# Gathering edge rows straight into an item's place, without the ring of tiles, in a graph transformer layer

## The chip, the cores and the metric

The kernel runs on one core of a Trainium2 chip. Its engines are TensorE (matrix products and transposes, PE in the rows), VectorE (DVE), ScalarE (ACT), GpSimd (POOL) and SyncE (SP, which here only issues DMAs); a small q behind a name means the engine's instruction queue. The metric is the device time of one execution in microseconds; the time before is the median of three runs.

## The reference

A graph layer over 6250 nodes of 128 features and 100,000 edges, sorted by their destination node. For each node k, q and v are its features times a matrix that its node type picks (eight types, each a mix of four basis matrices). For each edge k and v of its source node go through small matrices of its edge type (8 heads of 16), the score is the product of q at the destination with that k, times a factor of edge type and head; a softmax over the edges of a destination weighs v, the sums go through another matrix by node type, then come a product of the node's own features, a bias, ReLU, the residual and a layer norm:

```python
kt = jnp.einsum('nhi,thij->tnhj', k, relation_att)[edge_type, src]
e = (q[dst] * kt).sum(-1) * relation_pri[edge_type] * scale
a = softmax of e over the edges of one dst
vt = jnp.einsum('nhi,thij->tnhj', v, relation_msg)[edge_type, src]
agg = jax.ops.segment_sum(a[..., None] * vt, dst, num_segments=n)
out = relu(decomp(agg) + node_feat @ loop_weight + bias)
x = layernorm(x + out)
```

## The kernel before

**Table stage.** The nodes are taken in 49 blocks of 128 (a loop of 51 steps in TensorE's program). For each block and each of the eight edge types the finished k and v rows are made, copied out of PSUM by ScalarE (line 1557) into one of four places, and stored by SP (line 1141) in a table in HBM: 50,176 rows of 1 KB, one for each node and edge type. A block's store is 1 MB. ScalarE reuses a place once the store of four blocks earlier has landed. At block 41 SP first waits for five signals of stage 0, the last of which is GpSimd's clearing of agg (line 1435), and issues the loads for the queries (lines 1126, 1117, 1120).

**Setup beside it.** The edges lie in 782 tiles of 128 (784 with padding). A tile whose edges belong to more than one block of destination nodes counts once for each block: such a pair of tile and block is an item. There are 832 places for items, 26 groups of 32. GpSimd and VectorE work out which tile and which block an item has. Index gathers of GpSimd (line 1375, seven of them) fetch the destinations of each item, and TensorE turns two tables so that they lie by column (line 1883, in the steps 34, 35, 37 and 38): the lanes of the items, and the table rows of the tiles' edges, rows_idx. Clearing agg, whose space the first holds, waits for the turning.

**Query stage.** After the table q is made for all nodes by TensorE, ScalarE and VectorE.

**Loop over the groups.** For each item TensorE spreads the queries to the edges with a one-hot matrix, VectorE multiplies them with the k rows (line 686), four items (a batch) at a time, and sums them to scores (line 696); a group later the maxima are found, v is weighed (line 794), TensorE sums by node with the one-hot matrix (line 2084), and VectorE adds the sums to agg (line 845). The rows of the items lie in kv, which holds two groups, 64 items.

**How the rows get there.** GpSimd gathers each tile once, into one of the 16 places of a ring (lines 1448 to 1461). Before a gather it waits for the landing of the gather seven places back and passes that on to SP; for every second one it loads a count from a table and waits until SP has freed the ring's places. SP (bring, lines 1158 to 1175) loads the tile numbers of the batch's four items, waits until the place in kv is free, which is when the batch two groups back is weighed, waits for the tiles to have landed, and copies each item's tile from the ring to its place in kv:

```python
for u in range(4):
    if u == 2 and n > 0:
        sp.wait_ge(s_gathered[(n - 1) // NBATCH % 2][(n - 1) % NBATCH],
                   (n - 1) // (2 * NBATCH) * 64 + 64)
        sp.sem_inc(s_freed, 4)
    if u % 2 == 0:
        sp.wait_ge(s_landed, each[u + 1] & 1023)
        hold_apart(sp)
```

**Last stage.** The sums are normalised, multiplied, and stored. SP issues its loads; the first of these stand between its last copies.

The order on each engine is written out by hand; waits on semaphores join the engines.

Of the kernel before, what the change touches and what calls it, by code (L numbers as in the profile page):

```python
# [5 lines left out]
def graph_transformer_layer(  # L6
# [82 lines left out]
    RING = 16  # L89
    AHEAD = 7  # L90
    TSEMS = 8
    assert AHEAD < TSEMS and RING & (RING - 1) == 0 and GROUPS * G < ITEMS

# [7 lines left out]
    item_block = nc.dram_tensor("item_block", [2, ITEMS], i32, kind="Internal").ap()  # L101

    ctx = ExitStack()
    with ctx:
# [25 lines left out]
        rows_idx = sb("rows_idx", [P, TILES], i32)  # L130
# [4 lines left out]
        itile = strip[32:33, :].bitcast(i32)  # L135
        iblk = strip[64:65, :].bitcast(i32)
        starts_row = strip[96:97, 0:TILES - 1]
        next_start = starts_row.bitcast(i32)
# [6 lines left out]
        ring = sb("ring", [P, RING * 2 * D])  # L145
# [66 lines left out]
        s0i = rows3[:, 0:IPR * P].bitcast(i32)  # L212
        tdst = s0i[0:TROWS, :].rearrange("p (c e) -> p c e", c=TPR)
# [29 lines left out]
        yo = (s3.take(CN), ring[:, 0:CN])  # L243
# [15 lines left out]
        ring_coefs = take_coefs(Space(ring, RING * 2 * D, at=CN), HALF)  # L259
# [33 lines left out]
        s_stage0 = sem("s_stage0")  # L293
        s_items_turned = sem("s_items_turned")
# [13 lines left out]
        s_hold = sem("s_hold")  # L308
# [12 lines left out]

        s_tile = [sem(f"s_tile{r}") for r in range(TSEMS)]
        s_landed = sem("s_landed")
        s_freed = sem("s_freed")
# [74 lines left out]
        ITEMS_AT = [34, 35, 37, 38]  # L399
# [77 lines left out]

        def hold_apart(engine):


            engine.sem_inc(s_hold, 1)  # L481


        @block.vector
        def _(dve):
# [95 lines left out]
            def items():  # L581

                dve.wait_ge(s_column, IPR)
                did(v.tensor_scalar(fc[:, 0, :], fc[:, 0, :], -1.0, None, ALU.add))
                did(v.tensor_copy(ic[:, 0, :], fc[:, 0, :]), "item_tile")
                did(v.tensor_tensor(fc[:, 1, :], fc[:, 1, :], item_no[:, :], ALU.add))
                did(v.tensor_scalar(fc[:, 2, :], fc[:, 1, :], float(BLOCKS - 1), None, ALU.min))
                did(v.tensor_copy(ic[:, 1, :], fc[:, 2, :]))
                did(v.tensor_scalar(fc[:, 2, :], fc[:, 0, :], float(REAL - 1), 1.0, ALU.min, ALU.add))
                did(v.tensor_copy(ic[:, 2, :], fc[:, 2, :]))  # L590
                did(v.tensor_scalar(fc[:, 5, :], fc[:, 1, :], float(P), None, ALU.mult), "item_block")
# [13 lines left out]
            def copy_items(i):  # L605
# [6 lines left out]
                many = (P, TROWS)[a]  # L612
                for k in range(k0, k1):
                    v.tensor_copy(turned[:, k, :], PB[0][:, (k - k0) * P:(k - k0) * P + many])\
# [462 lines left out]
        def _(sp):  # L1077
# [73 lines left out]
            def tiles_of(i, count):  # L1151
                return nc.values_load_multi_w_load_instructions(  # L1152
                    itile[0:1, i:i + count], engines=(sp.engine,), min_val=1, max_val=REAL,
                    skip_runtime_bounds_check_because="clamped when written")[1]

            sp.wait_ge(s_item_blocks, 48)

            def bring(n):

                g, b = n // NBATCH, n % NBATCH  # L1160
                par = g % 2
                each = tiles_of(4 * n, 4)
                after(sp, s_weighted, g - 2, NBATCH, b + 1)
                for u in range(4):
                    if u == 2 and n > 0:
                        sp.wait_ge(s_gathered[(n - 1) // NBATCH % 2][(n - 1) % NBATCH],
                                   (n - 1) // (2 * NBATCH) * 64 + 64)
                        sp.sem_inc(s_freed, 4)  # L1168
                    if u % 2 == 0:
                        sp.wait_ge(s_landed, each[u + 1] & 1023)  # L1170
                        hold_apart(sp)
                    o = (par * G + b * 4 + u) * 2 * D
                    sp.dma_start(kv[:, o:o + 2 * D],  # L1173
                                 ring[:, bass.ds(((each[u] - 1) & (RING - 1)) * (2 * D), 2 * D)])\
                        .then_inc(s_gathered[par][b], 16)

            for n in range(12):
                bring(n)

# [20 lines left out]
            for n in range(12, 2 * NBATCH):  # L1200
                bring(n)
            for g in range(2, GROUPS):
                for b in range(NBATCH):
                    if g == GROUPS - 1 and b == NBATCH - 2:
                        sp.wait_ge(s_weighted, (GROUPS - 2) * NBATCH + 4)
                        sp.wait_ge(s_base_stored, 16 * (GROUPS - 4))
                        load_base(0)
                    if g == GROUPS - 1 and b == NBATCH - 1:
                        sp.wait_ge(s_item_sums, (GROUPS - 2) * 2 * NBATCH + HALF * NB // 2)
                        load_coefs(0, 0, HALF)  # L1210
                    bring(g * NBATCH + b)
# [78 lines left out]
        def _(pool):  # L1290
# [69 lines left out]
            did(g_.tensor_copy(next_start, tstart[96:97, 1:TILES]))  # L1360
# [18 lines left out]
            pool.dma_start(item_block.rearrange("a (p c) -> p a c", c=IPR), ic[:, 1:3, :]).then_inc(s_item_blocks, 16)  # L1379
            pool.wait_ge(s_item_blocks, 16)  # L1380
            pool.dma_start(iblk[:, :], item_block[0:1, :]).then_inc(s_item_blocks, 16)
            pool.dma_start(itile[:, :], item_block[1:2, :]).then_inc(s_item_blocks, 16)
# [61 lines left out]
            def landed(t):  # L1444
                pool.wait_ge(s_tile[t % TSEMS], t // TSEMS * 16 + 16)
                pool.sem_inc(s_landed, 1)

            for t in range(REAL):
                if t >= AHEAD:
                    landed(t - AHEAD)  # L1450
                if t >= RING and t % 2 == 0:
                    (done,) = nc.values_load_multi_w_load_instructions(
                        next_start[0:1, t + 1 - RING:t + 2 - RING], engines=(pool.engine,), min_val=1,
                        max_val=GROUPS * G, skip_runtime_bounds_check_because="counted from tiles")[1]
                    pool.wait_ge(s_freed, done & 1023)
                    hold_apart(pool)
                o = t % RING * 2 * D
                pool.indirect_dma_start(  # L1458
                    out=ring[:, o:o + 2 * D], out_offset=None, in_=table,
                    in_offset=bass.IndirectOffsetOnAxis(ap=rows_idx[:, t:t + 1], axis=0))\  # L1460
                    .then_inc(s_tile[t % TSEMS], 16)
            for t in range(REAL - AHEAD, REAL):
                landed(t)
# [383 lines left out]
        def _(pe):  # L1847
# [26 lines left out]
            def turn_items(i):  # L1874

                a, k0, k1 = ITEM_TURNS[i]
                if i == 0:
                    pe.wait_ge(s_lanes_rows, 1)
                bank_free()
                many = (P, TROWS)[a]  # L1880
# [387 lines left out]
```

## Time and profile before

| | us |
|---|---|
| median of three runs | 1298.71 (1298.19 to 1299.36) |
| span of the profiled execution | 1757.2 |
| table stage, until the first gather | 199.15 |
| busy: TensorE, VectorE, ScalarE, GpSimd | 1160.7, 986.6, 785.6, 881.5 |

The time of the profiled execution is known by its span, which is much longer than the time of the runs that were timed without a profile. In a row of the profile a group is given by line, engine and operation, then what is written from what, the count, the busy time and the mean of one, and the idle time ahead of it with what ended it. "Issue" is time in which an engine waits for nothing that the profile shows.

### The profile page before, as it was taken

How to read it: one execution, taken by the hardware profiler on the slowest of the kernel's cores; microseconds unless marked ns; L12 is line 12 of the kernel's file. 1: busy time of each engine (PE TensorE's matmuls, PEld its weight loads, DVE VectorE, ACT ScalarE, POOL GpSimd, SP SyncE). 2: the span in 40 equal slices, each digit the busy share in tenths (PEclk: the TensorE clock that was granted, in tenths of full speed). 3: DMA queues.
4: the chain of work that ended last, by engine and by line, in shares of the span. 5: the costliest groups of instructions: out<-in, count | busy, mean ns of one | idle time of the engine just before them, and what ended most of it. 6: DMA issues, size and time to landing. Idle time of an engine off the chain costs nothing.

```text
span 1757.2 us, 31429 instructions
## 1 busy us (share of the span) xinstructions
PE 1160.7 (66%) x6730; PEld 962.9 (55%) x6730; DVE 986.6 (56%) x2832; ACT 785.6 (45%) x2217; POOL 881.5 (50%) x915
## 2 busy tenths in 40 slices
PE   8989875657556565566566655566565666656698
PEld 5445434656545554455455554565455565545587
DVE  7877463555445555445555554455554566545677
ACT  4667454444434434443344343443444354434324
POOL 2775354555555554545454545455545554545233
PEclk9999997777677767876777667766777687777699
DMA  8878754555555555545455555555555555555675
GB/s 261 323 289 316 284 172 140 157 148 158 152 159 153 157 151 151 149 141 151 150 163 148 158 152 154 148 160 164 151 162 154 154 168 148 155 150 162 187 242 194
DMA packets 225149, 309.08 MB, mean 176 GB/s; under 512 B 32423, under 2 KB 191119, under 8 KB 217781
## 3 DMA queue, kind: packets, MB, share of 16 engines
q1 hardware_dynamic: 159996, 188.75, 30.6%
q0 software_dynamic: 38880, 106.25, 23.4%
q10 hardware_dynamic: 26088, 12.08, 2.4%
q8 instruction: 61, 1.00, 0.2%
q14 instruction: 124, 1.01, 0.2%
HBM read 139.52 MB, written 58.78 MB: 113 GB/s over the span
## 4 chain that ended last, share of the span: by engine, by line
SPq 34%; issue 31%; PE 12%; DVE 9%; another core or an unknown queue 7%; DMA 2%; DVEq 2%; ACT 1%; POOL 1%; POOLq 0%; ACTq 0%
SPq L1173 27%; PE pb L1900 4%; SPq L1152 2%; PE pb L1923 2%; DVE agg L845 2%; SPq L481 2%; SPq L1170 2%; DVEq L814 2%; DMA kv<-ring 2%; PE pb L2084 1%; SPq L1168 1%; PE pb L2190 1%; PE pb L2028 1%; DVE kv L541 1%
## 5 line engine op out<-in xcount | busy, mean ns | idle before, releaser
L1458 POOL DMA_INDIRECT ring<-table,rows_idx x782 | 745.8, 954 | 736.6 <-SPq L1168 452.5
L2084 PE MATMUL pb<-work,onehot 128*128 128x136 f32 x1664 | 367.5, 358 | 214.1 <-DVE agg L845 152.8
L845 DVE TENSOR_TENSOR agg<-agg,pb 128x136 f32 x832 | 241.8, 291 | 459.9 <-remote 291.8
L2084 PEld LDWEIGHTS pb<-work,onehot 128*128 128x128 f32 x1664 | 307.0, 254 | 242.0 <-issue 210.9
L1650 ACT ACTIVATE work<-pb 128x512 f32<-128x512 f32 x208 | 124.0, 596 | 549.6 <-remote 376.2
L2028 PE MATMUL pb<-q_all,work 128*128 x1664 | 301.0, 340 | 1.3 <-issue 0.8
L2028 PEld LDWEIGHTS pb<-q_all,work 128*128 128x128 f32 x1664 | 280.6, 253 | 7.6 <-issue 4.9
L1637 ACT ACTIVATE work<-lane,neg_lane 128x128 f32<-128x128 f32 x800 | 253.3, 390 | 0.6
L2012 PE MATMUL pb<-ident,onehot 128*128 128x128 f32 x832 | 174.5, 347 | 115.6 <-issue 60.2
L2012 PEld LDWEIGHTS pb<-ident,onehot 128*128 128x128 f32 x832 | 125.4, 180 | 136.0 <-issue 71.3
L686 DVE TENSOR_TENSOR kv<-kv,pb 128x512 f32<-128x512 f32 x208 | 141.5, 680 | 96.6 <-issue 41.7
L1670 ACT ACTIVATE pb<-work 128x32 f32<-128x32 f32 x200 | 42.9, 215 | 228.7 <-DVE work L779 129.0
L696 DVE TENSOR_REDUCE work<-kv 128x32 f32<-128x512 f32 x208 | 141.4, 680 | 0.4
L794 DVE TENSOR_TENSOR work<-kv,pb 128x512 f32<-128x512 f32 x200 | 136.2, 681 | 5.7 <-ACT work L1671 3.8
L1644 ACT ACTIVATE onehot<-work 128x512 f32<-128x512 f32 x200 | 125.9, 630 | 6.3
L1557 ACT ACTIVATE kv<-pb 128x512 f32<-128x512 f32 x190 | 98.5, 602 | 43.1 <-PE pb L1923 38.8
L1900 PE MATMUL pb<-work,kv 128*128 128x512 f32 x196 | 108.1, 634 | 8.3 <-DVE kv L541 6.9
L541 DVE SCALAR_TENSOR_TENSOR kv<-pb,onehot,kv 128x128 f32<-128x128 f32 x294 | 80.4, 341 | 0.4 <-PE pb L1900 0.2
L2057 PE MATMUL pb<-ones,end_out 1*128 1x1 f32 x208 | 41.8, 318 | 53.3 <-DVE end_out L758 19.6
L2048 PE MATMUL pb<-ident,work 128*1 128x128 f32 x104 | 20.4, 332 | 82.9 <-DVE work L731 55.0
L2057 PEld LDWEIGHTS pb<-ones,end_out 1*128 1x128 f32 x208 | 39.6, 280 | 61.7 <-DVE end_out L758 21.5
L1923 PE MATMUL pb<-onehot,kv 32*128 32x256 f32 x784 | 60.1, 401 | 1.5 <-issue 0.9
(239 smaller groups left out, 1237.2 us busy)
## 6 DMA issues: line engine op xcount, KB each, us to landing
kv<-ring SPq DMA_DIRECT2D x832, 128.0 KB
table<-kv SPq DMA_DIRECT2D x49, 1024.0 KB, 5.2
ring<-table,rows_idx POOLq DMA_INDIRECT x782
kv<-base_rows SPq DMA_DIRECT2D x7, 448.0 KB, 7.6
kv<-in_x_dram SPq DMA_DIRECT2D x8, 384.0 KB, 5.8
seg<-item_bias ACTq DMA_DIRECT2D x48, 64.0 KB
base_rows<-pair ACTq DMA_DIRECT2D x24, 128.0 KB
onehot<-coef_rows SPq DMA_DIRECT2D x3, 1024.0 KB, 5.5
```

Of the source, the lines that this page charges most:

```text
L686: v.tensor_tensor(rows_of(par, b)[:, :, 0:D], rows_of(par, b)[:, :, 0:D], PB[2 + b % 2][:, :].rearrange("p (u d) -> p u d", u=4), ALU.mult)\
L696: v.tensor_reduce(sc[:, :, l0:l0 + 4].rearrange("p h l -> p l h"), rows_of(par, b)[:, :, 0:D].rearrange("p u (h k) -> p u h k", h=H), AX.X ...
L794: v.tensor_tensor(w[:, :, 0:D].rearrange("p u (h k) -> p u h k", h=H), rows.rearrange("p u (h k) -> p u h k", h=H), weights_of(b).unsqueez ...
L845: v.tensor_tensor(a, a, PB[banks[i // 2 % len(banks)]][:, (i % 2) * 256:(i % 2) * 256 + W], ALU.add).then_inc(s_added, 1)
L1173: sp.dma_start(kv[:, o:o + 2 * D], ring[:, bass.ds(((each[u] - 1) & (RING - 1)) * (2 * D), 2 * D)])\
L1458: pool.indirect_dma_start(out=ring[:, o:o + 2 * D], out_offset=None, in_=table, in_offset=bass.IndirectOffsetOnAxis(ap=rows_idx[:, t:t + 1 ...
L1637: square = a_.activation(sq[:, u, :], lane[:, :], ACT.Square, bias=neg_lane[:, bass.ds(g * G + b * 4 + u, 1)])
L1644: a_.activation(onehot[:, o:o + 4 * P], sq[:, :, :].rearrange("p u e -> p (u e)"), ACT.Relu, bias=1.0, scale=-1.0).then_inc(s_one_hot, 1)
L1900: t_.matmul(PB[2 + half][:, :], xT[:, c * P:(c + 1) * P], Bkv[:, 2 * half:2 * half + 2, :, :].rearrange("p b k d -> p (b k d)"), start=Tru ...
L2012: mm = t_.transpose(PB[0][:, u * P:(u + 1) * P], onehot[:, o:o + P], ident[:, :])
L2028: mm = t_.matmul(PB[2 + b % 2][:, u * D:(u + 1) * D], spread[:, b % 2, u, :], q_all[:, bass.ds(blks[u] * D, D)], start=True, stop=True)
L2084: mm = t_.matmul(PB[banks[k % len(banks)]][:, u * 256:u * 256 + W], onehot[:, o:o + P], wv[:, b % WR, h * 2 + u, :], start=True, stop=True)
```

## The change

The ring, its two-sided signals and SP's copies go. GpSimd issues one gather for each item, 832 of them, from the table into the item's place in kv. Ahead of the four gathers of a batch it waits until the place is free (the batch two groups back is weighed), and for the landing of the batch two places back. For that the rows of an item's edges have to be known by item: the sources are stored in HBM by tile (tile_sources), GpSimd fetches them by item with seven more index gathers, and TensorE turns that table. The two last turnings move from the steps 37 and 38 to 43 and 44. The space of the ring that the last stage used is now an own tensor, late.

```diff
-        rows_idx = sb("rows_idx", [P, TILES], i32)
+        rows_idx = sb("rows_idx", [P, ITEMS], i32)
...
-        ITEMS_AT = [34, 35, 37, 38]
+        ITEMS_AT = [34, 35, 43, 44]
...
-            for n in range(12):
-                bring(n)
...
-            g_.tensor_tensor(srcf, srcf, etf, ALU.add).then_inc(s_lanes_rows, 1)
+            did(g_.tensor_tensor(srcf, srcf, etf, ALU.add))
+            pool.sem_inc(s_lanes_rows, 1)
+            pool.dma_start(tile_sources.rearrange("(p c) e -> p (c e)", c=TPR), srcf).then_inc(s_sources_stored, 16)
             pool.wait_ge(s_item_keys, 32)
             pool.dma_start(krow, item_keys.rearrange("(a k) i -> a k i", a=1)).then_inc(s_item_keys, 16)
+            pool.wait_ge(s_sources_stored, 16)
+            for k in range(IPR):
+                pool.indirect_dma_start(
+                    out=item_sources[:, k * P:(k + 1) * P], out_offset=None, in_=tile_sources,
+                    in_offset=bass.IndirectOffsetOnAxis(ap=ic[:, 0, k:k + 1], axis=0)).then_inc(s_item_sources, 16)
...
-            for t in range(REAL):
-                if t >= AHEAD:
-                    landed(t - AHEAD)
-                if t >= RING and t % 2 == 0:
-                    (done,) = nc.values_load_multi_w_load_instructions(
-                        next_start[0:1, t + 1 - RING:t + 2 - RING], engines=(pool.engine,), min_val=1,
-                        max_val=GROUPS * G, skip_runtime_bounds_check_because="counted from tiles")[1]
-                    pool.wait_ge(s_freed, done & 1023)
-                    hold_apart(pool)
-                o = t % RING * 2 * D
-                pool.indirect_dma_start(
-                    out=ring[:, o:o + 2 * D], out_offset=None, in_=table,
-                    in_offset=bass.IndirectOffsetOnAxis(ap=rows_idx[:, t:t + 1], axis=0))\
-                    .then_inc(s_tile[t % TSEMS], 16)
+            for g in range(GROUPS):
+                for b in range(NBATCH):
+                    after(pool, s_weighted, g - 2, NBATCH, b + 1)
+                    n = g * NBATCH + b - 2
+                    if n >= 0:
+                        pool.wait_ge(s_gathered[n // NBATCH % 2][n % NBATCH], n // (2 * NBATCH) * 64 + 64)
+                    for u in range(4):
+                        i = b * 4 + u
+                        o = (g % 2 * G + i) * 2 * D
+                        pool.indirect_dma_start(
+                            out=kv[:, o:o + 2 * D], out_offset=None, in_=table,
+                            in_offset=bass.IndirectOffsetOnAxis(ap=rows_idx[:, g * G + i:g * G + i + 1], axis=0))\
+                            .then_inc(s_gathered[g % 2][b], 16)
...
+                if a == 1:
+                    pe.wait_ge(s_item_sources, 16 * IPR)
...
-            pe.wait_ge(s_item_blocks, 48)
+            pe.wait_ge(s_item_blocks, 32)
```

## Rows read from the trace of the kernel before

**Rows 1.** The page: span, busy time of each engine, the costliest group of instructions.

```profile
span 1757.2 us, 31429 instructions
...
PE 1160.7 (66%) x6730; PEld 962.9 (55%) x6730; DVE 986.6 (56%) x2832; ACT 785.6 (45%) x2217; POOL 881.5 (50%) x915
...
L1458 POOL DMA_INDIRECT ring<-table,rows_idx x782 | 745.8, 954 | 736.6 <-SPq L1168 452.5
```

**Rows 2.** Line 1173, 1643.5 to 1660 us; ns of one: least, median, most.

```profile
L1173 SPq ALU_OP  x28: 37/37/37, 1643.9 to 1659.4; - x28
...
L1173 SPq DMA_DIRECT2D kv<-ring x15: 16/486/510, 1643.7 to 1659.6; - x15
```

**Rows 3.** Timeline of SP, 1643 to 1660 us; start, us in all, count.

```profile
1643.72 5.43 SPq L1173 DMA_DIRECT2D kv<-ring  x7
```

**Rows 4.** Chain that ended last, from 799 us on; start, us, what.

```profile
799.38 0.70 SPq L1170
800.10 0.71 SPq L481
...
804.50 0.73 SPq L1173
```

**Rows 5.** Timeline of GpSimd, until the sixteenth gather; in brackets idle time before.

```profile
91.54 0.97 POOL L1375 DMA_INDIRECT agg<-tile_rows,onehot  x1 [0.30 <-issue]
...
121.29 0.58 POOL L1405 DMA_DIRECT2D agg<-item_keys  x1
...
154.70 5.65 POOL L1435 MEMSET agg<- 128x6664 f32 x1 [3.71 <-DMA band<-agg]
199.15 1.06 POOL L1458 DMA_INDIRECT ring<-table,rows_idx  x1 [38.80 <-DMA table<-kv]
200.51 0.98 POOL L1458 DMA_INDIRECT ring<-table,rows_idx  x1 [0.30 <-issue]
...
218.11 0.95 POOL L1458 DMA_INDIRECT ring<-table,rows_idx  x1 [0.31 <-issue]
```

**Rows 6.** Busy time of each engine in the loop's stretch.

```profile
266.30:1664.00 1397.70, 844.45 (x4712) 762.33 (x4712) 727.72 (x1982) 594.35 (x1766) 707.90 (x743) 0.74 0.52 154
```

**Rows 7.** Timeline of GpSimd and VectorE at the loop's end: last gather, last product.

```profile
1641.63 1.05 POOL L1458 DMA_INDIRECT ring<-table,rows_idx  x1 [0.30 <-issue]
...
1663.68 0.69 DVE L686 TENSOR_TENSOR kv<-kv,pb 128x512 f32<-128x512 f32 x1
```

**Rows 8.** Instructions on the ring: the gathers' ns, and landings of its DMAs.

```profile
L1458 POOL DMA_INDIRECT ring<-table,rows_idx x782: 947/949/1302, 199.2 to 1641.6; - x196
...
DMA to landing us min/median/max: 3.0/3.8/8.9
```

**Rows 9.** Timeline of VectorE: query stage, first product, first weighing.

```profile
219.29 0.35 DVE L669 SCALAR_TENSOR_TENSOR q_all<-pb,onehot,q_all 128x128 f32<-128x128 f32 x1 [9.33 <-issue]
...
266.34 0.69 DVE L686 TENSOR_TENSOR kv<-kv,pb 128x512 f32<-128x512 f32 x1 [3.97 <-PE pb L2028]
...
312.69 0.67 DVE L794 TENSOR_TENSOR work<-kv,pb 128x512 f32<-128x512 f32 x1
```

**Rows 10.** Timeline of TensorE, SP and ScalarE at the table stage's end.

```profile
152.05 0.45 PE L1883 MATMUL pb<-ident,onehot 112*128 112x112 f32 x3
...
169.04 0.49 PE L1856 MATMUL pb<-ident,kv 128*128 128x128 f32 x3
...
169.54 2.13 SPq L1126 DMA_DIRECT2D onehot<-in_L_gnn_w_basis_q_dram  x1
...
173.42 1.38 SPq L1120 DMA_DIRECT2D onehot<-in_x_dram  x1
174.85 18.29 SPq L1141 DMA_DIRECT2D table<-kv  x8
...
183.57 2.07 ACT L1557 ACTIVATE kv<-pb 128x512 f32<-128x512 f32 x4 [0.92 <-PE pb L1923]
```

**Rows 11.** A stretch of the table stage's end; last columns: granted clock, DMA share, GB/s.

```profile
185.00:190.00 5.00, 4.23 (x37) 2.40 (x36) 3.92 (x12) 3.11 (x8) 0.00 (x0) 1.00 1.00 410
```

More of the change, by code:

```diff
@@ L88, in graph_transformer_layer @@
     REAL = -(-E // P)
[L89 to L92, printed above, removed]
+    assert GROUPS * G < ITEMS
     table = nc.dram_tensor("table", [NP * T, 2 * D], f32, kind="Internal").ap()
@@ L144, in graph_transformer_layer @@
         kv = sb("kv", [P, 2 * G * 2 * D])
-        ring = sb("ring", [P, RING * 2 * D])
+        late = sb("late", [P, CN + 4 * NB * P])
         onehot = sb("onehot", [P, 2 * G * P])
@@ L242, in graph_transformer_layer @@
         y = [s3.take(CN) for _ in range(2)]
-        yo = (s3.take(CN), ring[:, 0:CN])
+        yo = (s3.take(CN), late[:, 0:CN])
         an = [s3.take(CN) for _ in range(2)]
@@ L258, in graph_transformer_layer @@
         even_coefs = take_coefs(q3, CB)
-        ring_coefs = take_coefs(Space(ring, RING * 2 * D, at=CN), HALF)
+        ring_coefs = take_coefs(Space(late, CN + 4 * NB * P, at=CN), HALF)
         first_coefs, odd_coefs = take_coefs(h3, HALF), take_coefs(h3, HALF)
@@ L293, in graph_transformer_layer @@
         s_stage0 = sem("s_stage0")
+        s_sources_stored = sem("s_sources_stored")
+        s_item_sources = sem("s_item_sources")
         s_items_turned = sem("s_items_turned")
@@ L320, in graph_transformer_layer @@
         s_q_terms = sem("s_q_terms")
-        s_tile = [sem(f"s_tile{r}") for r in range(TSEMS)]
-        s_landed = sem("s_landed")
-        s_freed = sem("s_freed")
         s_segments = [sem(f"s_segments{r}") for r in range(2)]
@@ L476, in after @@
             engine.wait_ge(s, base * per + k)
-        def hold_apart(engine):
-            engine.sem_inc(s_hold, 1)
         @block.vector
@@ L588, in items @@
                 did(v.tensor_copy(ic[:, 1, :], fc[:, 2, :]))
-                did(v.tensor_scalar(fc[:, 2, :], fc[:, 0, :], float(REAL - 1), 1.0, ALU.min, ALU.add))
-                did(v.tensor_copy(ic[:, 2, :], fc[:, 2, :]))
                 did(v.tensor_scalar(fc[:, 5, :], fc[:, 1, :], float(P), None, ALU.mult), "item_block")
@@ L1149, in _ @@
                         .then_inc(s_segments[g], 16)
[L1151 to L1175, printed above, removed]
-            for n in range(12):
-                bring(n)
             def load_base(ch):
@@ L1199, in _ @@
                          x[0:2 * P, :].rearrange("(c p) d -> p c d", p=P)).then_inc(s_pair_loaded, 16)
[L1200 to L1211, printed above, removed]
+            sp.wait_ge(s_weighted, (GROUPS - 2) * NBATCH + 4)
+            sp.wait_ge(s_base_stored, 16 * (GROUPS - 4))
+            load_base(0)
+            sp.wait_ge(s_item_sums, (GROUPS - 2) * 2 * NBATCH + HALF * NB // 2)
+            load_coefs(0, 0, HALF)
             whole = BLOCKS - 1
@@ L1878, in turn_items @@
                     pe.wait_ge(s_lanes_rows, 1)
+                if a == 1:
+                    pe.wait_ge(s_item_sources, 16 * IPR)
                 bank_free()
-                many = (P, TROWS)[a]
-                each = (lanes, srcf.rearrange("p (c e) -> p c e", c=TPR))[a]
+                each = (lanes, item_sources.rearrange("p (c e) -> p c e", c=IPR))[a]
                 for k in range(k0, k1):
-                    t_.transpose(PB[0][:, (k - k0) * P:(k - k0) * P + many], each[:, k, :],
-                                 ident[0:many, 0:many]).then_inc(s_items_turned, 1)
+                    t_.transpose(PB[0][:, (k - k0) * P:(k - k0 + 1) * P], each[:, k, :],
+                                 ident[:, :]).then_inc(s_items_turned, 1)
                 bank0.append((s_items_copied, a * IPR + k1))
```

22 lines of the change are left out of this document (6 added, 16 removed).

## The prediction

> **What bounds the kernel now.** I read the busy totals first: no engine is busy for more than 66% of a span of 1757.2 us [rows 1]. The times of the three runs have a median of 1298.71 us, 458 us less than that span, so the recorded execution is not the one that is timed, and the next question is which part of it is stretched. The costliest group is GpSimd's gather into the ring: 782 of them, 745.8 us busy, and nearly as long idle before them, 452.5 us of it for SP's line 1168, which is the release of ring places [rows 1]. So the recording says that SP holds GpSimd up. The look at SP itself says why that can't be taken over: in the stretch from 1643.5 us the register operations of line 1173 take 37 ns and a copy's issue 486 ns [rows 2], and seven items go through in 5.43 us [rows 3]; from 799 us on the chain is one SP instruction after another at 0.70 us each, register operations and waits alike [rows 4]. An ALU operation of 37 ns that takes 700 ns is recording cost on the queue with the most instructions. I take the fast stretch for the timed execution: some 0.78 us an item, 24.8 us for a group of 32.
>
> With SP taken out, GpSimd's own pace is left. A gather lasts 0.95 us and the next starts 0.30 us after its end, also where nothing waits [rows 5]: the first sixteen, which need no released place, run from 199.15 to 218.11 us in this beat. The seven index gathers of line 1375, with no instruction at all between them, keep the same gap, so the 0.30 us belongs to the gather and not to the waits and register loads between two of them. A gather costs 1.255 us, 782 cost 981.4 us, 37.7 us a group on the mean. The other engines need less: in the 1397.7 us of the loop VectorE is busy 727.7, ScalarE 594.4 and TensorE 844.5 us at a granted clock of 0.74 [rows 6], that is 28.0, 22.9 and 32.5 us for each of 26 groups.
>
> The check on this reading: the first gather at 199.15, 981.4 us of gathers, then some 12 us until the last batch's product (estimate: the last eight or nine items at 0.78 us and a landing of 3.8 us; the recorded lag is 21.0 us, from the last gather's end at 1642.68 to the product at 1663.68 [rows 7]), and 93.5 us from there to the span's end at 1757.2. Sum 1286 us against 1298.71. The 12.7 us left are stalls of the ring's handshake and what lies around the span; which of the two, the trace can't say.
>
> **The change part by part.** *More gathers.* One gather for each item in place of one for each tile: 832 for 782, 50 x 1.255 = +62.7 us on the path that sets the end. VectorE, ScalarE and TensorE do what they did; SP loses the 832 copies and their register work, GpSimd the signals of landings and the loads of ring places, and none of this was in its 1.255 us. So I give nothing for them, except the handshake's stalls: between 0 and 12.7 us are won back, I take half, 6.
>
> *The wait for the batch two places back.* Before the first gather of a batch, the last gather of the batch two back must have landed; it was issued five places earlier, 5 x 1.255 = 6.27 us. Landings of the ring's transfers take 3.0 to 8.9 us, 3.8 in the median [rows 8]. Behind this wait stand the batch's four gathers and everything later on GpSimd, and VectorE's product waits for those. At the median it costs nothing; if every landing took the longest value, 2.6 us at each of 206 batches, 541 us. I take 0, from the median, since the ring's copies, which share the DMA engines in the recording, are gone.
>
> *The wait for a free place in kv.* It was SP's, behind a ring of 16; now it is GpSimd's, which can run 64 gathers ahead of the first weighing and not 80. 64 gathers are over 80.3 us after the first, at 287 us by the start worked out below. The recording has the first weighing at 312.7 us, 46.4 us after the first product [rows 9], both behind the slow stretches. A stall here would come once, at most 26 us with that row, 0 if the timed execution reaches the weighing by 287 us. I take 0: the query stage ahead of it also shows all engines halted together, VectorE 9.33 us for nothing it waits for [rows 9], which the timed run doesn't have. Later batches are weighed a group ahead.
>
> *The setup.* A store of the sources, a wait for it, and seven more index gathers, 7 x 1.25 us, move GpSimd's chain from 121.29 us on by some 9.5 us. It had 38.80 us of idle time ahead of the first gather [rows 5], so that alone is hidden. But the turning of the item tables moves from the steps 37 and 38 of TensorE's loop to 43 and 44, and the clearing of agg (5.65 us) waits for it [rows 5]. SP waits for the clearing ahead of table block 41. Step 38's transposes are at 152.05, x's for step 43 at 169.04 us; with a step of 3.4 us step 44's come at 172.4 [rows 10]. Clearing then ends near 178.7. SP behind it issues the query loads, which took from 169.54 to 174.80 us, so block 41's store goes out near 184.1 and not at 174.85. Queued behind are the stores of 42 to 48; ScalarE's copy for block 45, at 183.57 us, waits for 41's place. In this stretch the DMA engines are full, share 1.00 at 410 GB/s [rows 11]: a block's 1.05 MB takes 2.6 us and eight stores some 20 us, so the lost time isn't made up, except for the 1.2 MB of query loads (2.8 us at most), which now pass while the queue is empty. 9.2 us later at the issue less some 1.7 us: +7.5 us on the first gather, at 206.6. Between 4 (only ScalarE's wait) and 9.2.
>
> *The end.* The last gather lands in kv itself, 3 us after its end, in place of 12 us over SP: -9, between 0 and -18.
>
> Sum: 206.6 + 832 x 1.255 = 1250.8; + 3 + 93.5 = 1347.3; + half of the unexplained 12.7 = 1353.6. Forecast **1353 us**, 54 over the median. The profile's own span should shrink at the same time, from 1757 to under 1420, since SP's slowed instructions leave the path.
>
> **A rule against it.** The 782 gathers last 947 ns at the least, 949 in the median, 1302 at the most, beside a VectorE that is busy in half of the loop [rows 6, 8]. The Trainium skill, in "SBUF — State Buffer", section "SBUF: two separate sides", says that descriptors written by GpSimd's cores stop while VectorE holds the shared port pair. By that rule more gathers would also be longer gathers. The trace doesn't agree for these float32 operations: median and least differ by 2 ns.
>
> **The rivals.** (a) *The 0.30 us are recording cost.* Then a gather takes 0.95 us, 30.4 us a group, and the ring's handshake or a chain over VectorE set the 38 us a group that the time implies. For it: all other recorded gaps of SP are inflated. Against it: the gap is 0.30 or 0.31 us in slow and in fast stretches, and 981 us fill the time almost without rest. It decides at a beat below (1298.7 - 206.6 - 96.5 - 6) / 832 = 1.19 us: below that the change is faster. With 0.95 us the gathers take 790 us, and the busiest engine in the loop, TensorE with 844.5 us [rows 6] from the first product at about 255, ends at 255 + 845 + 93.5 = 1194 us at the best; if a chain over the other engines was the limit, only the setup and the end move, 1299 + 7.5 - 9 = 1297. I set 0.12: 0.08 to faster, 0.04 to no change. (b) *The landings are late.* Gathers straight into kv compete with VectorE's reads of kv and eight in flight are not enough: at 6.8 us, some way past the middle between the median and the longest value [rows 8], each batch loses 0.5 us, 206 batches 109 us, 1462 us. Decides from 6.27 us. For it, 8.9 us occurs; against it, the gaps of 0.30 us under a limit of seven in flight. 0.07. (c) *The stall at the first free place* of up to 26 us: 1380 us, 0.10. (d) *Gathers lengthen beside VectorE's operations* once it runs without the record's halts: at the longest gather of the record [rows 8], 0.35 us more on each of 832, 1353 + 291 = 1644 us; 0.01, since 0.949 us is the value in busy and idle stretches alike. It is what the Trainium skill's rule above would make of the time.
>
> **How the numbers follow.** Forecast 0.70, with its own range 1337 to 1368: the setup's 4 to 9.2, the end's 0 to -18, the rest's 0 to 12.7 us. Case (c) lengthens the range upwards to 1376; below it I go to 1322, where a beat of 1.217 us would end. Outside lie (a), (b), (d) and the longest stalls of (c). About 0.2% is what a measurement of this kernel can tell from no change. Faster 0.08 and same 0.04 are case (a), slower 0.88 the rest.
>
> **What would show it.** Right: gathers at 0.95 us with 0.30 us between them nearly without break from about 206 us on, and SP gone from the chain. The first gather at 199 us would refute the setup's step; gaps of over 1 us before each fourth gather, ended by a landing, speak for (b); one long gap before the 65th for (c); unbroken gathers and yet a time below 1300 us for (a), and then the forecast is wrong altogether.

## The result, and the profile after

| | before | after |
|---|---|---|
| median, in the runs made side by side | 1299.03 us (1298.19 to 1300.89) | 1344.15 us (1343.03 to 1345.23) |
| ratio, 95% interval | | 1.0335 [1.0313, 1.0357] |

The change costs 45 us. The page of the kernel after, whose own time was 1343.03 us, so that 1.7 us lie around its span; it answers to [rows 1], and its chain of waits to [rows 4]:

```profile
span 1341.3 us, 25172 instructions
...
PE 1037.7 (77%) x6730; PEld 848.8 (63%) x6730; DVE 986.0 (74%) x2830; ACT 784.8 (59%) x2217; POOL 936.4 (70%) x971
...
POOL 34%; issue 24%; PE 20%; DVE 12%; DMA 4%; ACT 4%; DVEq 2%; ACTq 0%; SPq 0%; POOLq 0%
...
L1407 POOL DMA_INDIRECT kv<-table,rows_idx x832 | 795.3, 956 | 281.0 <-issue 247.4
```

No engine is busy for more than 77% of the span, and yet one of them sets the time. GpSimd's 795.3 us of gathers and the 281.0 us of idle time ahead of them belong together: 811 of those idle times are "issue" and none of them is long. Both halves stand at the head of the chain (34% and 24%), where SP's instructions stood in the record of [rows 4]. The waits of GpSimd show it (line waiting, what for: us in all, times, longest):

```profile
POOL kv L1407 <- issue: 247.4, 811, 0.3
...
POOL kv L1407 <- DMA table<-kv: 27.5, 1, 27.5
...
POOL kv L1407 <- DVE work L779: 3.7, 12, 0.3
...
POOL kv L1407 <- DMA kv<-table,rows_idx: 2.4, 8, 0.3
```

After the wait for the table (27.5 us, once) nothing is longer than 0.3 us: neither the free place in kv (12 times, VectorE's line 779), nor the landing two batches back (8 times), holds GpSimd for longer than the gap that lies between any two gathers. GpSimd's timeline, setup and loop (start, us, what, in brackets the idle time before), against [rows 5, 7]:

```profile
120.69 0.62 POOL L1352 DMA_DIRECT2D tile_sources<-onehot  x1 [0.61 <-POOL onehot L1350]
...
125.57 1.06 POOL L1357 DMA_INDIRECT agg<-tile_sources,onehot  x1 [3.73 <-DMA tile_sources<-onehot]
126.93 0.97 POOL L1357 DMA_INDIRECT agg<-tile_sources,onehot  x1 [0.30 <-issue]
...
165.33 5.65 POOL L1389 MEMSET agg<- 128x6664 f32 x1 [6.45 <-PE pb L1831]
198.46 1.02 POOL L1407 DMA_INDIRECT kv<-table,rows_idx  x1 [27.47 <-DMA table<-kv]
199.78 0.95 POOL L1407 DMA_INDIRECT kv<-table,rows_idx  x1 [0.30 <-issue]
...
1246.36 0.95 POOL L1407 DMA_INDIRECT kv<-table,rows_idx  x1 [0.31 <-issue]
```

From 198.46 to 1246.36 us lie 831 steps, 1.261 us each; the median step is 1.254. The gathers themselves, least, median and most in ns, and their landings, against [rows 8]:

```profile
L1407 POOL DMA_INDIRECT kv<-table,rows_idx x832: 949/949/1305, 198.5 to 1246.4; - x167
...
  DVE kv L671: 152.9, 90
...
DMA to landing us min/median/max: 2.7/2.8/4.0
```

The middle line is new in kind: who waited for these gathers. VectorE's product of k and q stood still for 152.9 us at 90 batches until rows landed. And a stretch of the loop (busy us and count of TensorE, its weight loads, VectorE, ScalarE, GpSimd; granted clock, share of the DMA engines, GB/s), against [rows 6]:

```profile
248.00:1248.00 1000.00, 729.34 (x4698) 650.98 (x4696) 726.96 (x1974) 591.69 (x1762) 757.70 (x793) 0.85 0.41 116
```

793 gathers in 1000 us, and the DMA engines are busy for 41% of it.

### The profile page after: what moved, and what is told of

Its sections match the earlier page's. It is cut to its first block, busy times and chain, and to the rows that moved or that the text cites. A ratio compares the mean times of both kernels' runs of the same rounds, so it can differ in the third digit from the quotient of the medians.

```text
span 1341.3 us, 25172 instructions
## 1 busy us (share of the span) xinstructions
PE 1037.7 (77%) x6730; PEld 848.8 (63%) x6730; DVE 986.0 (74%) x2830; ACT 784.8 (59%) x2217; POOL 936.4 (70%) x971
## 4 chain that ended last, share of the span: by engine, by line
POOL 34%; issue 24%; PE 20%; DVE 12%; DMA 4%; ACT 4%; DVEq 2%; ACTq 0%; SPq 0%; POOLq 0%
POOL kv L1407 34%; PE pb L1848 5%; PE pb L1871 3%; PE pb L1928 3%; DMA kv<-table,rows_idx 3%; DVE agg L830 2%; PE pb L1976 2%; PE pb L2032 2%; ACT work L1584 1%; DVEq L799 1%; PE pb L1960 1%; DVE kv L529 1%; DVE work L779 1%; ACT onehot L1591 1%; PE pb L2138 1%
## 5 line engine op out<-in xcount | busy, mean ns | idle before, releaser
L1407 POOL DMA_INDIRECT kv<-table,rows_idx x832 | 795.3, 956 | 281.0 <-issue 247.4
L2032 PE MATMUL pb<-work,onehot 128*128 128x136 f32 x1664 | 320.8, 322 | 112.0 <-DVE agg L830 85.7
L2032 PEld LDWEIGHTS pb<-work,onehot 128*128 128x128 f32 x1664 | 262.2, 221 | 138.7 <-issue 88.8
L1976 PE MATMUL pb<-q_all,work 128*128 x1664 | 266.5, 312 | 0.5 <-DVE q_all L654 0.2
L671 DVE TENSOR_TENSOR kv<-kv,pb 128x512 f32<-128x512 f32 x208 | 141.9, 682 | 161.6 <-DMA kv<-table,rows_idx 152.9
L1976 PEld LDWEIGHTS pb<-q_all,work 128*128 128x128 f32 x1664 | 242.7, 223 | 9.1 <-issue 4.2
L1960 PE MATMUL pb<-ident,onehot 128*128 128x128 f32 x832 | 148.4, 307 | 49.7 <-ACT onehot L1591 47.2
L1960 PEld LDWEIGHTS pb<-ident,onehot 128*128 128x128 f32 x832 | 107.6, 158 | 65.8 <-ACT onehot L1591 62.2
L1848 PE MATMUL pb<-work,kv 128*128 128x512 f32 x196 | 105.1, 618 | 6.2 <-DVE kv L529 4.7
L2005 PE MATMUL pb<-ones,end_out 1*128 1x1 f32 x208 | 34.6, 283 | 41.3 <-DVE end_out L743 41.3
L2005 PEld LDWEIGHTS pb<-ones,end_out 1*128 1x128 f32 x208 | 32.3, 233 | 49.3 <-DVE end_out L743 49.3
```

The source lines that it names most:

```text
L671: v.tensor_tensor(rows_of(par, b)[:, :, 0:D], rows_of(par, b)[:, :, 0:D], PB[2 + b % 2][:, :].rearrange("p (u d) -> p u d", u=4), ALU.mult)\
L1407: pool.indirect_dma_start(out=kv[:, o:o + 2 * D], out_offset=None, in_=table, in_offset=bass.IndirectOffsetOnAxis(ap=rows_idx[:, g * G + i ...
L1848: t_.matmul(PB[2 + half][:, :], xT[:, c * P:(c + 1) * P], Bkv[:, 2 * half:2 * half + 2, :, :].rearrange("p b k d -> p (b k d)"), start=Tru ...
L1960: mm = t_.transpose(PB[0][:, u * P:(u + 1) * P], onehot[:, o:o + P], ident[:, :])
L1976: mm = t_.matmul(PB[2 + b % 2][:, u * D:(u + 1) * D], spread[:, b % 2, u, :], q_all[:, bass.ds(blks[u] * D, D)], start=True, stop=True)
L2032: mm = t_.matmul(PB[banks[k % len(banks)]][:, u * 256:u * 256 + W], onehot[:, o:o + P], wv[:, b % WR, h * 2 + u, :], start=True, stop=True)
```

## The kernel before, recorded again

The first thing to settle was the ground on which the forecast stood: a record of 1757.2 us for a kernel that takes 1299.

**Before, unchanged, with a new profile.** No edit.

> The kernel before, unchanged, with a profile of its own. Theory (SP's instructions of 0.7 us and the span of 1757 us belong to that one recording): a span within 10 us of 1298, register operations of SP at 37 ns throughout, gathers in a beat of 1.255 us, and single rests that sum up to some 12 us, ended by SP's release or by a landing. Rival (recording always stretches a kernel with so many SP instructions): a span above 1700 us again.

Measured, in one run: 1297.93 us with a span of 1295.7, 2.2 us around it. Its page, the waits of GpSimd in it, and three rows of its timeline of GpSimd and one of VectorE's:

```profile
span 1295.7 us, 31429 instructions
...
PE 1019.2 (79%) x6730; PEld 831.1 (64%) x6730; DVE 985.4 (76%) x2832; ACT 783.3 (60%) x2217; POOL 878.5 (68%) x915
...
L1458 POOL DMA_INDIRECT ring<-table,rows_idx x782 | 743.5, 951 | 277.4 <-issue 175.4
```

```profile
POOL ring L1458 <- issue: 175.4, 568, 2.2
POOL ring L1458 <- DMA ring<-table,rows_idx: 50.9, 167, 0.3
...
POOL ring L1458 <- SPq L1168: 21.1, 46, 2.0
```

```profile
192.16 1.06 POOL L1458 DMA_INDIRECT ring<-table,rows_idx  x1 [29.98 <-DMA table<-kv]
...
1141.98 0.95 POOL L1458 DMA_INDIRECT ring<-table,rows_idx  x1 [2.21 <-issue]
...
1182.16 0.95 POOL L1458 DMA_INDIRECT ring<-table,rows_idx  x1 [0.30 <-issue]
...
1203.73 0.69 DVE L686 TENSOR_TENSOR kv<-kv,pb 128x512 f32<-128x512 f32 x1
```

What follows: of the 452.5 us for which GpSimd waited for SP in [rows 1] 21.1 are left, so the 1757 us were that one record's; why it was so long stays open. The beat of 1.25 us is not that record's; it fills the loop of the kernel before as well, and the bound named in the prediction holds for its gathers. Three things could not be seen in the stretched record: the first gather comes at 192.16 and not at 199.15 us; GpSimd rests nine times for 9.5 us in all beyond the 0.305 us, all of it in the last 300 us of the gathers; and the last product still comes 20.6 us after the last gather's end (1183.11 to 1203.73), where I had estimated 12 for a record without the slowed SP.

A second bound lies close beside the first, and the prediction did not see it. The chain that ended last in this record runs through SP's copies (34%) far more than through GpSimd's gathers (4%, their landings 11%), and SP's own waits say why:

```profile
DMA kv<-ring 34%; DMA ring<-table,rows_idx 11%; SPq L1173 9%; PE pb L1900 6%; POOL ring L1458 4%; PE pb L1980 3%; PE pb L1923 3%; PE pb L2190 1%; POOLq L1452 1%; DVE agg L845 1%; DVE kv L541 1%; DVEq L814 1%; PE pb L1909 1%; PE pb L2028 1%; PE pb L2084 1%
```

```profile
SPq L1168 <- DMA kv<-ring: 141.7, 179, 3.1
...
SPq L481 <- POOLq L1446: 26.2, 33, 4.5
```

SP waits 141.7 us for its copies to land and only 26.2 us for GpSimd's gathers, 0.7 of it after 750 us: the copying, with all that it waits for, runs hardly faster than the gathers. So in the kernel before the two are nearly tied, GpSimd with 9.5 us of rests in 991 and the copies right behind it. That GpSimd is the slower of the two is shown below by the 50 gathers more.

With that, every record, those of the experiments below too, can be cut into the same three pieces: until the first gather, from it to the end of the last, and from there to the end of the span (all in us, from the timeline of GpSimd; rests are what goes beyond the 0.305 us between two gathers; records with the same setup have their first gather within 3.7 us).

| record | first gather | gathers, their stretch | rests | after the last | span |
|---|---|---|---|---|---|
| before, again | 192.2 | 782, 991.0 | 9.5 | 112.6 | 1295.7 |
| before, six ahead | 194.9 | 782, 991.3 | 6.6 | 108.9 | 1295.0 |
| before, four ahead | 194.0 | 782, 1044.6 | 63.3 | 104.6 | 1343.1 |
| before, 50 more | 195.9 | 832, 1045.6 | 0.1 | 104.1 | 1345.6 |
| after | 198.5 | 832, 1048.9 | 0.1 | 94.0 | 1341.3 |
| after, three back | 198.1 | 832, 1047.7 | 0.1 | 96.4 | 1342.2 |
| after, queries later | 195.8 | 832, 1046.1 | 0.0 | 95.8 | 1337.7 |
| after, 50 fewer | 198.7 | 782, 983.3 | 0.1 | 96.4 | 1278.4 |
| after, half the rows | 198.0 | 832, 1013.3 | 0.1 | 96.2 | 1307.5 |
| after, one back | 198.1 | 832, 1529.3 | 485.8 | 95.0 | 1822.4 |

Taking the mean of the first two rows as before and of "after" and "three back" as after, the change is +4.8 us ahead of the gathers, +57.2 in them and -15.6 behind them: +46.4 us of span.

## The experiments on the gathers

**After, with 50 gathers fewer.** 50 items, spread over the groups from the third on, are not gathered (their rows are what the place held; the waits count without them), so the kernel has as many gathers as the one before.

```diff
...
+                        if g * G + i in left_out:
+                            continue
                         pool.indirect_dma_start(
...
```

> The changed kernel with 782 gathers in place of 832: 50 items from group 2 on, every fifteenth, are not gathered and keep what lay in their place. Everything else is as in the changed kernel. Theory (GpSimd's gather beat of 1.255 us sets the loop): 1344 - 63 = 1281 us, so below the kernel before, and the rest of the difference between the two kernels is some 18 us in favour of the change. Rival (the wait for landings or the place in kv sets the loop, and the number of gathers is by the way): 1335 us or more. Rival (VectorE's chain is nearly as slow as the gathers): a gain that stops half way, above 1300 us.

Measured: 1277.73 us (1277.14 to 1280.13), 0.983 [0.9795, 0.9866] of before, and 66.4 us under the kernel after. The stretch of the gathers is 65.6 us shorter, 1.31 for each that is left out: the whole price of a gather is on the path, and nothing else takes its place. This is also where the change's gain would show: with as many gathers as before, though not with the layer's result, direct gathers take 1.7% less than ring and copies (1.3 to 2.1%).

**Before, with 50 gathers more.** Fifty extra gathers into a spare place, of 128 rows of 256 bytes in place of 1 KB, in a kernel that keeps ring, SP's copies and the old setup.

```diff
...
+                if t in more:
+                    if t > min(more):
+                        pool.wait_ge(s_spare, 16 * sum(m < t for m in more))
+                    pool.indirect_dma_start(
+                        out=spare[:, :], out_offset=None, in_=table.rearrange("r (k d) -> (r k) d", k=4),
+                        in_offset=bass.IndirectOffsetOnAxis(ap=rows_idx[:, t:t + 1], axis=0)).then_inc(s_spare, 16)
```

> The kernel before with 50 more index gathers of GpSimd, each of 128 rows of 256 bytes into a spare place, one after every fourteenth tile from the 65th on. Theory (the kernel before is set by the gather beat too in the timed execution): 1299 + 63 = 1362 us, or down to 1349 if the ring's handshake left GpSimd idle for up to 13 us. Rival (SP's handshake set the loop before, as its profile says): no more than 1310 us, since GpSimd would have the time.

Measured: 1348.72 us (1346.87 to 1351.49), 1.0384 [1.0345, 1.0423] of before, at the lower end of the 1349 to 1362 expected: the number of gathers alone makes a kernel as slow as the change does. Its groups of gathers and the waits of those on the ring (count | busy, mean ns | idle before):

```profile
L1461 POOL DMA_INDIRECT ring<-table,rows_idx x782 | 745.0, 953 | 274.0 <-issue 175.8 <-DMA ring<-table,rows_idx 54.6 <-DMA table<-kv 36.0
L1468 POOL DMA_INDIRECT spare<-table,rows_idx x50 | 47.3, 946 | 15.2 <-issue 10.7 <-DMA ring<-table,rows_idx 3.4 <-SPq L1170 1.2
```

```profile
POOL ring L1461 <- issue: 175.8, 577, 0.3
POOL ring L1461 <- DMA ring<-table,rows_idx: 54.6, 179, 0.3
```

The extra 50 cost 62.5 us of GpSimd (47.3 + 15.2), the time rises by 50.5: some 12 us were absorbed. The table shows by what: the rests (9.5 or 6.6 us before, 0.1 here) and a shorter way from the last gather to the end (104.1 against 108.9 and 112.6). With GpSimd 62.5 us slower SP waits 134.1 us for it, 154 times, in place of 26.2 us and 33 times: the copies have become the faster of the two:

```profile
SPq L483 <- POOLq L1448: 134.1, 154, 5.7
```

A gather of a quarter of the bytes takes as long, 946 ns.

**After, with half the rows in each gather.** From the third group on a gather brings 64 rows in place of 128; the other half of an item's edges keeps what the place held.

```diff
+                        rows = P if g < 2 else P // 2
                         pool.indirect_dma_start(
-                            out=kv[:, o:o + 2 * D], out_offset=None, in_=table,
-                            in_offset=bass.IndirectOffsetOnAxis(ap=rows_idx[:, g * G + i:g * G + i + 1], axis=0))\
+                            out=kv[0:rows, o:o + 2 * D], out_offset=None, in_=table,
+                            in_offset=bass.IndirectOffsetOnAxis(ap=rows_idx[0:rows, g * G + i:g * G + i + 1], axis=0))\
```

> The changed kernel with gathers of 64 rows in place of 128 from group 2 on: the upper 64 edges of each item keep what lay there. The engines behind do the same work. Theory (a gather's 0.95 us goes with its rows): some 0.5 us busy and a beat of 0.8 us, so the chain over VectorE sets the loop, 33 us a group as in the changed kernel's groups 1 and 2, and the time falls to 1160 to 1200 us. Rival (the price is one of the instruction): the beat stays 1.25 us, 1344 us.

Measured: 1309.16 us (1307.32 to 1310.23), 1.0055 [1.0036, 1.0074] of before. Both expectations missed, the rival's by less. The gathers by ns, and two neighbours in the timeline:

```profile
L1408 POOL DMA_INDIRECT kv<-table,rows_idx x832: 896/903/1302, 198.0 to 1210.4; - x167
```

```profile
704.23 0.91 POOL L1408 DMA_INDIRECT kv<-table,rows_idx  x1 [0.30 <-issue]
705.44 0.90 POOL L1408 DMA_INDIRECT kv<-table,rows_idx  x1 [0.31 <-issue]
```

903 ns for 64 rows, 949 for 128: 0.72 ns a row and, by these two points, an estimated 0.857 us for the instruction without any, and the gap stays. 768 shorter gathers by 0.046 us are 35.3 us, and the time fell by 35.0. So between 64 and 128 rows the price goes nearly by the instruction, and the time follows it to the microsecond.

## The experiments on the waits

**After, waiting for the batch one place back.**

```diff
-                    n = g * NBATCH + b - 2
+                    n = g * NBATCH + b - 1
```

> The changed kernel, waiting ahead of a batch for the landing of the batch one place back, not two. Theory (the wait costs only what a landing takes beyond the gathers issued meanwhile, 5 of them at two places back, 1 here): a landing of 2.8 us against 1.255, so 1.5 to 2.0 us at each of 207 batches, 1655 to 1760 us. Rival (gathers land in the order of issue well ahead of what the profile gives, and the wait is free at any place): 1344 us.

Measured: 1825.38 us (1824.15 to 1826.61), 1.4026 [1.3981, 1.4071] of before. Waits of GpSimd, and the landings of its gathers:

```profile
POOL kv L1407 <- DMA kv<-table,rows_idx: 537.9, 206, 3.8
POOL kv L1407 <- issue: 201.3, 625, 2.8
```

```profile
DMA to landing us min/median/max: 2.6/2.8/5.2
```

The direction was expected, the size was above it: a batch now waits 2.6 us (537.9 / 206) where the gap of 0.30 would stand, 2.3 us more, 475 us in all, and the time is 481 us longer. The expectation took the landing of 2.8 us less one beat, some 1.5 us. What it lacked is the way from a landing to the next gather's start, 0.7 us in the median of the 156 batches whose landing is on record. So the wait in the change is a real one, and its place decides: from one place back it would cost 481 us.

**After, waiting for the batch three places back.**

```diff
-                    n = g * NBATCH + b - 2
+                    n = g * NBATCH + b - 3
```

> The changed kernel with the wait ahead of a batch's four gathers put on the batch three places back instead of two. My theory: the wait two places back costs nothing, since landings of the changed kernel take 2.8 us in the median and 4.0 at the most, and the landing waited for has had five beats of 1.254 us, 6.27 us; then the time stays at 1344 us within 0.3% (1340 to 1348), and the gathers keep a beat of 1.25 us. Rival: the wait does hold GpSimd a little at each batch, hidden in the 0.30 us between two gathers; then three places back give back up to 0.1 us on each of 206 batches, 20 us, and the time is 1324 to 1338 us.

Measured: 1343.49 us (1341.71 to 1344.32), beside 1344.15 for the change; the stretch of the gathers is 1047.7 us against 1048.9. The runs of the kernel before that were made beside the two have medians of 1294.89 and 1299.03 us, so it is the stretches, and the waits shown above (2.4 us in eight of them), that decide: the wait two places back costs nothing that can be seen.

**Before, with four gathers in flight in place of seven.**

```diff
-    AHEAD = 7
+    AHEAD = 4
```

> The kernel before with the landing of a gather passed on to SP after four more gathers, not seven. Theory (of the 12.7 us that my sum for the kernel before left unexplained most is the ring's handshake): places come free 3.8 us earlier, 1288 to 1295 us. Rival (the rest lies around the span or in the gathers, and the ring never held GpSimd up): 1299 us, within 2; slower if a landing takes longer than four beats, 5.0 us.

Measured: 1345.45 us (1343.53 to 1358.27), 1.0374 [1.0332, 1.0416] of before; the theory missed, and only the rival's last clause named the direction. Waits of GpSimd:

```profile
POOL ring L1458 <- issue: 173.9, 510, 2.8
POOL ring L1458 <- DMA ring<-table,rows_idx: 119.9, 253, 2.5
```

I had reckoned with the median landing of [rows 8], 3.8 us, under the 5.0 us of four beats. But no landing of [rows 8] is a gather's. The view of the ring lists none for them; its 3.0, 3.8 and 8.9 us come from four transfers of the last stage, three stores and one load, as the issues from 1660 us on in that record show (KB each, us to landing):

```profile
out_dram<-ring SPq DMA_DIRECT2D x3, 448.0 KB, 3.0
ring<-coef_rows SPq DMA_DIRECT2D x1, 1024.0 KB, 8.9
```

The gathers' landings can be read from the 16 signals that each of them sends. Of the gathers with all 16 on record, 570 of 782 in this run, the median landed 3.5 us after its start and the last 6.0; 14 took over 5.0 us. In the new record of before it is 3.6 and 6.3 us (478 gathers). So long landings alone do not make this run's 63.3 us of rests. A gather that had to wait starts not with the landing but 0.8 us after it, and 1.4 us after it where GpSimd also loads the count of freed places, ahead of every second gather (medians of 18 and 46 of the waiting gathers). 60 of the 86 rests are of that second kind. At 64 of the 86 the landing is on record, and at 58 of these it took less than 5.0 us. The loss of time, 47 us, is less than the rests, since the end comes 4 to 8 us sooner after the last gather and the rests of the kernel before are among the 63.3. Beside SP's copies a gather does land later, 3.5 to 3.6 us in the median against 2.8 in the kernel after; with six beats between, this costs next to nothing.

**Before, with six in flight.** The same line with 6.

> The kernel before with the landing passed on after six more gathers, not seven. Four gave 1345 us, with GpSimd waiting for landings 253 times, so landings beside the ring's copies take about 5 us and more. Theory (at seven GpSimd rests for the ring's release, at four for landings, and between them lies a best place): 1290 to 1297 us. Rival (at seven GpSimd's rests are landings too, the longest of them): 1302 to 1312 us.

Measured: 1301.32 us (1296.09 to 1304.46), 0.9993 [0.9977, 1.001] of before: no difference, and its rests of 6.6 us are no more than the 9.5 with seven. It lies between the two expectations, and neither came.

## The experiment on the setup

**After, with the query loads four blocks later.** SP then issues block 41's store without waiting for GpSimd's clearing of agg.

```diff
-        TILES_AT, STARTS_AT, BIAS_AT, QUERIES_AT = 4, 9, 24, BLOCKS - 8
+        TILES_AT, STARTS_AT, BIAS_AT, QUERIES_AT = 4, 9, 24, BLOCKS - 4
```

> The changed kernel with the query loads, and SP's wait for the clearing ahead of them, four table blocks later (at block 45 in place of 41). Theory (the setup's moved turning costs time through SP's wait): ScalarE's wait of 5.2 us for a table store goes and the first gather comes 4 to 8 us earlier, 1336 to 1340 us. Rival (the DMA engines set the end of the table stage anyway, and the wait only moves work about): 1344 us, within 2.

Measured: 1339.42 us (1338.40 to 1341.66), 1.0308 [1.0279, 1.0336] of before; against the kernel after the first gather comes 2.3 to 2.6 us sooner and the time is 4.7 us less, though the two intervals overlap. So the time expected came and ScalarE's wait went, but the first gather gained less than the 4 to 8 us expected, and half of the 4.7 us has no cause shown. SP's issues and ScalarE's copies in the kernel after, which answer to [rows 10], show what was moved away:

```profile
171.01 0.38 SPq L1111 DMA_DIRECT2D onehot<-in_L_gnn_w_basis_q_dram  x1
...
173.05 0.54 SPq L1105 DMA_DIRECT2D onehot<-in_x_dram  x1
173.64 18.48 SPq L1126 DMA_DIRECT2D table<-kv  x8
```

```profile
180.35 2.06 ACT L1504 ACTIVATE kv<-pb 128x512 f32<-128x512 f32 x4 [5.18 <-DMA table<-kv]
```

SP issues its loads at 171.01, in the moment the clearing is done (165.33 + 5.65 = 170.98), the eight stores go out from 173.64, and ScalarE waits 5.18 us for a place. In the new record of before the same eight go out from 168.07 and that wait isn't there:

```profile
168.07 19.27 SPq L1141 DMA_DIRECT2D table<-kv  x8
```

```profile
176.81 2.06 ACT L1557 ACTIVATE kv<-pb 128x512 f32<-128x512 f32 x4 [0.92 <-PE pb L1923]
```

None of the versions that compute the whole layer is faster than the kernel before.

## Why the prediction was right, and where it was off

The forecast was 1353 us, measured were 1344. The mechanism was the one that happened: 832 unbroken gathers. The stated range, 1337 to 1368, is a little narrower than the sum of its terms, 1335 to 1371.

*What bounds, and the beat.* Right. 1.255 us was read from sixteen gathers ahead of the loop; 1.254 is the median step of the 831 in it, and the stretch of 832 gathers is 1047.7 to 1048.9 us against 1044.2 forecast. The 4 us over that are the few long ones: in the profiled execution 24 gathers took over 1 us, 5 us more in all.

*More gathers, less the ring's stalls.* Right in size. +62.7 less 6 was the forecast, +57.2 is measured. The 12.7 us left unexplained, of which half was laid to the ring, are in the new record 6.6 to 9.5 us of rests, 2.2 us around the span, and a remainder; two other terms of that check, the first gather's time (too late) and the way from the last gather to the end (too short), were wrong in opposite directions and all but hid each other, which was luck. That SP needs 24.8 us a group left out its waits: in the new record it waits 141.7 us for its copies to land, and its path is nearly as slow as GpSimd's.

*The wait two places back: 0.* Right, by the experiments with one and three places. The reason given rested on a row read wrongly: the 3.0 to 8.9 us of [rows 8] are stores and a load of the last stage, and no gather's landing was among them, so the 541 us at worst and the 6.8 us of rival (b) had no ground in it either. What the runs show, where landings are on record (156 of the 832 in the kernel after): the gathers land after 2.8 us in the median and 4.0 at the most, and up to 5.3 in the records of its other versions. With the 0.7 us from a landing to the next start this stays under 6.27, at the longest by a quarter of a microsecond.

*A free place in kv: 0.* Right; no wait for VectorE's weighing was over 0.3 us.

*The setup.* The chain of it was right link by link: the store and seven gathers shift GpSimd (the first gather of line 1357 after 3.73 us of waiting), the clearing waits for the turning, SP for the clearing, the stores for SP, ScalarE for the stores. Its size was +7.5, within 4 to 9.2; measured are 3.2 to 6.3 between the pairs of records, 4.8 on the mean, and 4.0 on the mean of all records with the old setup and the new one (without the query loads' move), at the foot of the range. The five loads took 2.6 us of issue in place of the 5.3 of [rows 10] and of the new record of before.

*The first gather's time: the term that failed most.* I put the +7.5 on 199.15 us [rows 5] and got 206.6; it came at 198.46. I had rejected the record's loop as stretched and still took its table stage as good. It was 3 to 7 us late there as well: the four new records with the old setup have the first gather at 192.2 to 195.9. With the setup's size this makes 8 of the 9 us by which the forecast was high. I had also written that a first gather at 199 would refute the setup's step; against those four records it does not.

*The end.* Forecast -9, measured -15.6. The new end is as forecast, 94.0 to 96.4 us after the last gather against 96.5 (3 + 93.5). The old one was longer than I thought, 108.9 to 112.6 against 105.5: when the last gather is done, twelve items are still to be copied in the new record and not eight or nine, and SP's first loads for the last stage, one behind a wait of 3.5 us, stand between these copies. With 50 more gathers the rests go, eight copies are left, and the last product comes 13.7 us after the last gather in place of 20.6. That the copies fall behind because their path is nearly as slow as the gathers' is read from the waits of SP; no run tried it.

*What lies around the span.* 1.7 us, where the sum carried 6.

Of the rivals, (a) fell with the first experiments: the 0.30 us are paid without any record, since 50 gathers fewer take 66 us off the time of runs that nothing recorded. (b), (c) and (d) have no row: no wait for a landing or a place over 0.3 us, and a median gather of 949 ns as before. VectorE is busy in 727 of 1000 us of the loop of the kernel after, and least and median of the gathers are the same 949 ns. The Trainium skill ("SBUF — State Buffer", section "SBUF: two separate sides") has GpSimd's descriptors stop only beside VectorE operations that take the shared port pair: those in a 2-port mode, or with two inputs in SBUF against a GpSimd operation that reads SBUF. The products here read one input from SBUF and one from PSUM (kv and pb in the rows), and no run shows a 2-port mode, so the even 949 ns do not speak against the rule; the prediction's "doesn't agree" and its rival (d) took it too widely.

## What to carry to other kernels

Count a GpSimd gather by the instruction: 1.255 us from one to the next here, as much for a quarter of the bytes and 1.21 for half the rows, so that an edit that halves the bytes moved in the loop and removes 832 copies still loses by 50 gathers. Where the profiled execution is much longer than the timed runs, doubt each absolute time in it and not only those in the stretched part, and forecast the difference that the edit makes on the measured time. A wait on a landing is free so long as the issues in between take longer than the longest landing under that load and the 0.7 us and more from a landing to the next start; take the longest and not the median, and see first whose landings a view lists.

## What the runs showed of the hardware

- The indirect gather: 949 ns for 128 rows of 1 KB, 946 for 128 of 256 bytes, 903 for 64 of 1 KB (an estimated 0.857 us and 0.72 ns a row by these), then 0.305 us until the next one begins.
- Landings of gathers: 2.8 us in the median and 4.0 to 5.3 at the most in the records without SP's copies (share of the DMA engines 0.41 in the loop of the kernel after), 3.5 to 3.6 and up to 6.3 beside SP's copies inside SBUF (share 0.78).
- From a landing that GpSimd waited for to the start of the next gather: 0.7 us with one batch back, 0.8 with four tiles back, 1.4 where a count is loaded in between.
- One record of a kernel can be 460 us longer than the kernel, with register operations of 37 ns on a chain whose steps take 0.7 us; the next record of the same kernel was 2.2 us under the time of its own run.
